# Local attention on one core: TensorE multiplies the values of chunk n-4 before it turns chunk n-3

## The reference, cut to what matters

```python
def _L0_attn_ref(x, wq, wkv, wo, q_norm_w, k_norm_w):
    q = x @ wq.T                      # 16 query heads of 64
    kv = x @ wkv.T                    # one key head, one value head
    ...
    q = _rmsnorm(_rope(q), q_norm_w)
    k = _rmsnorm(_rope(k), k_norm_w)
    mask = (cols <= rows) & (rows - cols <= WINDOW)     # WINDOW = 128
    scores = jnp.einsum('bqgtd,bqgsd->bqgts', q, k) * scale
    scores = jnp.where(mask[None, None, None], scores, NEG)
    attn = jax.nn.softmax(scores, axis=-1)
    out = jnp.einsum('bqgts,bqgsd->bqgtd', attn, v)
    ...
    return out @ wo.T
```

## Time and profile before

| | |
|---|---|
| median of three executions | 912.0 us (903.77 to 914.52) |
| the profiled execution | 905.44 us, of which the span of the instructions is 902.8 us |
| mean granted clock of TensorE | 0.900 of full speed |
| busy: PE, DVE, ACT, POOL | 739.3, 607.1, 448.7, 429.4 us |
| chunks of local attention | 4 images x 32 = 128 |

### The profile page before, as it was taken

The page is one execution under the profiler, slowest core; times in us unless marked ns, Lnnn a source line. Parts: engine busy times, 40 slices in busy tenths (PEclk is TensorE's granted clock), DMA queues, the critical chain, the costliest instruction groups (busy, mean ns, idle before and its releaser), DMA issues. The chain is left out here.

```text
span 902.8 us, 21152 instructions
## 1 busy us (share of the span) xinstructions
PE 739.3 (82%) x8196; PEld 484.5 (54%) x8196; DVE 607.1 (67%) x1209; ACT 448.7 (50%) x1405; POOL 429.4 (48%) x556
## 2 busy tenths in 40 slices
PE   6699999899998989988789979987899986405880
PEld 6243776426774447763267734773577753303660
DVE  0478887588885988876878836676577759512870
ACT  0024999127994359972299925312666650101100
POOL 0655666274662656643656612662033230472675
PEclk9889999999999999999999998997999997556755
DMA  7353000170000710001200000008000004017000
GB/s 253 118 204 73 3 3 3 46 219 14 2 4 1 233 45 3 3 3 29 62 2 3 3 1 1 1 3 110 8 3 2 2 2 129 27 44 129 9 18 14
DMA packets 60008, 41.30 MB, mean 46 GB/s; under 512 B 51760, under 2 KB 57389, under 8 KB 59124
## 3 DMA queue, kind: packets, MB, share of 16 engines
q1 hardware_dynamic: 57462, 33.03, 14.5%
q10 hardware_dynamic: 144, 4.19, 1.2%
q0 software_dynamic: 2304, 2.74, 0.9%
HBM read 25.44 MB, written 7.15 MB: 36 GB/s over the span
## 5 line engine op out<-in xcount | busy, mean ns | idle before, releaser
L795 ACT ACTIVATE work<-ps,small,rq 128x160 f32<-128x160 f32 x512 | 242.8, 487 | 31.9 <-DVE small L741 31.4
L774 POOL TENSOR_TENSOR work<-work,small 128x512 f32<-128x512 f32 x128 | 133.1, 1040 | 123.9 <-DVE small L758 123.9
L738 DVE TENSOR_REDUCE ps<-ps 128x4 f32<-128x640 f32 x128 | 106.5, 832 | 40.5 <-PE ps L648 39.2
L795 ACT ACTIVATION_READ_ACCUMULATOR work<-ps,small,rq 128x1 f32 x512 | 105.3, 206 | 0.0
L648 PE MATMUL ps<-kT,big 64*128 64x160 f32 x1024 | 97.8, 311 | 0.0
L750 DVE COPY pT<-ps 128x640 f32<-128x640 f32 x116 | 95.5, 823 | 0.5 <-issue 0.5
L683 PE MATMUL ps<-pT,vwin 128*64 128x128 f32 x1024 | 84.2, 282 | 9.7 <-ACT big L783 2.4
L273 PE MATMUL ps<-xT,s_proj_w 64*128 64x512 f32 x288 | 78.6, 663 | 12.6 <-PEq L213 7.5
L608 POOL TENSOR_TENSOR big<-prod 128x1024 f32<-128x1024 f32 x28 | 65.8, 2361 | 27.4 <-DVE prod L575 27.2
L648 PEld LDWEIGHTS ps<-kT,big 64*128 64x128 f32 x1024 | 76.1, 191 | 0.1
L683 PEld LDWEIGHTS ps<-pT,vwin 128*64 128x64 f32 x1024 | 56.7, 136 | 23.6 <-issue 17.6
(11 more groups left out here) (284 smaller groups left out, 1425.8 us busy)
## 6 DMA issues: line engine op xcount, KB each, us to landing
xb<-in_x SPq DMA_DIRECT2D x3, 4096.0 KB, 14.0
xb<-in_x ACTq DMA_DIRECT2D x1, 4096.0 KB, 18.0
vrem<-hl SPq DMA_DIRECT2D x64, 64.0 KB, 2.1
sent_rows<-empty_row SPq DMA_DIRECT2D x8, 325.0 KB, 9.9
s_proj_w<-in_proj_w SPq DMA_DIRECT2D x1, 1536.0 KB, 6.1
big<-sent_rows SPq DMA_DIRECT2D x5, 264.0 KB, 5.2
big<-sent_rows SPq DMA_DIRECT2D x5, 256.0 KB, 4.6
xb<-in_ffn_w SPq DMA_DIRECT2D x1, 1028.0 KB, 4.6
```

What stands on the lines that cost most here:

```text
L738: ch.step(v.tensor_reduce(row_max(c), ps[:, s_banks(c), 0:2 * SPAN].rearrange("p e (h k) -> p e h k", h=2), X, ALU.max))
L774: g.tensor_tensor(probs[:, c % 3, :, 0:P], probs[:, c % 3, :, 0:P], bc(small[:, c % 4, 3, :], P), ALU.mult)
L795: nc.scalar.activation(probs[:, c % 3, q, :], bank[2 * (c % 2) + e][:, SPAN * hh:SPAN * hh + SPAN], ACT.Exp, bias=small[:, c % 4, 1, q:q + ...
```

## The change

Inside PE's loop the two calls change places. No instruction is added or removed, and no wait either; the waits that belong to a call move with it. `values(n - 4)` now comes after `scores(n)`, and `turn(n - 3)` comes last.

```diff
                         pe.wait_ge(S["x_loaded"], 16 * VALUE_LOADS)
                         if b + 1 < IMAGES:
                             pe.wait_ge(S["next_kept"], 1)
+                    if n >= 4:
+                        values(n - 4)
                     if 3 <= n < CHUNKS + 3:
                         turn(n - 3)
-                    if n >= 4:
-                        values(n - 4)
                 pe.wait_ge(S["oT_ready"], CHUNKS)
```

## The result

The changed kernel takes 1030.71 us (median of four, 1029.45 to 1033.95), beside 912.84 for the kernel before (four executions, 903.77 to 914.52). The ratio is 1.134, with a 95% interval of 1.129 to 1.139. The profiled execution took 1031.31 us with a span of 1029.5, which is 126.7 more than the 902.8 before; 98 were forecast.

The account below looks back on a forecast made before the run. The prediction took ACT to bound the kernel's steady part, PE close behind. It added 4 x (21.8 + 0.2 + 2.5) = 98 us to the profiled 905.4, giving 1003.5, and named 1007 us, range 988 to 1035.

Parts of the forecast that it names:

- the loop: Local attention's steady part: a cycle of waits through PE and ACT, once a chunk, binds; 993 to 1020 us, chance 83%.
- the end of an image: From q0 of chunk 31 to the output projection: 10.50 us where it was 7.97, +2.5 an image.
- the step: Time from one chunk's q0 to the next, chunks 4 to 31: 2.99 us where 2.184 was, 21.8 us an image.
- ACT's idle time: Sign: ahead of q0 ACT idles some 0.8 us a chunk, put down to PE's turn.
- the first image's local attention: Sign: image 0's local attention longer by 24 us, the experts onward unchanged.
- PE's idle time: Sign: ahead of the values PE idles about 0.5 us a chunk, put down to ACT's output copy.
- The clock rival: Rival: PE's clock falls in the gaps of the steady chunks, +56 us, 1063 us; chance 10%.
- Chunks 0 to 4: Start of each image: q0 of chunk 4 also waits for values and turn; 0.2 us an image, 0.8 in all.
- Only PE's order costs: Rival: in the steady chunks no loop closes; 2.31 us a chunk, about 921 us; chance 4%.
- Not slower: Rival: the steady chunks stay at 2.184 us with ACT the bound, about 905 to 912 us; chance 3%.

Follow-up runs that it names:

- e1: Changed kernel with ACT's output copy ahead of q0, where it stood between q1 and q2; 950.12 us, ratio to before 1.050.
- e2: Changed kernel with four buffers for the exponentials in place of three, so q0 waits for the turn of n-4; 945.66 us, ratio 1.046.
- e3: Changed kernel with products that nothing reads in PE's gaps after the last scores of each image; 1010.63 us, ratio to before 1.119.
- e6: Kernel before up to n = 31, with the changed order (values first) only from n = 32 on; 933.38 us, ratio 1.025.
- e5: Changed kernel with the new order only for n from 4 to 31, the old order (turn first) after; 1004.23 us, ratio 1.102.

## Why the prediction was right in direction and too small

Forecast were 1007 us and, for the loop, 993 to 1020; measured were 1030.71. That lies in the wide range of 988 to 1035, and in the stretch that the prediction gave to a falling clock (1020 to 1118) with a chance of 10%. The step that failed is the end of an image: the prediction put it at 10.50 us with the clock at 1.00 and the projection behind it at no change. It took 13.86 us at a clock of 0.54, and the projections took 7.6 us more in sum. Of the signs that the prediction named, the step and ACT's idle time came true; the end of an image, and the first image's local attention, forecast 24 us longer and 29.8 longer from its first q0 to L714, did not.

**The mechanism** was right, piece by piece. The loop q0, q1, output copy, values, turn, q0 is what binds; the timeline shows its pieces at 1.32, 0.14, 0.96 and 0.63 against 1.31, 0.15, 0.97 and 0.56; and it went when either wait was met early (e1, e2), and shrank by one exponential when one was taken out of it. DVE's copy and the scores were covered, and ACT idles 0.81 ahead of q0, as forecast. PE's idle time was not: 0.91 us a step where some 0.5 was forecast, since the scores end 0.55 after q0 and not 0.9. That costs nothing by itself, but the argument on the clock rested on it.

**The step** was sized at 2.99 and measured 3.053. The whole difference is the last piece: the 0.56 had been read from ACT's half copy (L803), which waits for the turn first and for the values second. Ahead of q0 the turn is the second wait, and that costs 0.06. Exchanging the waits brought 2.993. Over 108 steps this is 6.5 us. The range allowed for it (3.06), the middle value did not. The wait list of the two instructions, not only the engine and the releaser, has to be alike where a hand-over is carried from one row to another.

**The end of an image** is the step that failed. The count of its rounds was right: with the clock held at 1.00 (e3) it takes 10.34 us, forecast 10.50. A round there takes 2.39 and not 2.50, mostly because the output copy starts 0.34 behind the half copy and not 0.44, and the first half copy starts 0.18 later than forecast. But the forecast put all of it at the full clock, and at 0.5 it takes 13.86, and the projection behind it, forecast unchanged, begins at the low clock and takes 2 us more. That is 12.6 us at the ends and about 7.5 behind them, 20 of the 28 us missed. e3 shows the cause: it only puts products, and one wait for the bank that they use, into PE's gaps, and the clock stays at 1.00. What e3 leaves open is how much the thinner steady steps ahead of the gap add to it.

**The clock rival** was placed wrongly. I looked for it in the steady loop, where PE waits 0.91 us in 3.05 and the clock stayed 1.00. There the argument against it was unsound and the outcome luck: I had PE busy 2.4 of 3 us, more than in the earlier trace rows, but it is busy 13.65 of 20, less than the 3.76 of 5 of those rows. And I argued from the kernel before's own ends, where gaps of 0.50 and 0.60 had left it at 1.00. The ends of the changed kernel have no scores between values and turn, and gaps of 1.56 and 0.90 that my own sum contained (1.46 behind q0 for the first values, then half copy, output copy and hand-over each time) and that I never held against those 0.50 and 0.60. The page "TensorE: Matmul & The Clock Gate" of the Trainium skill, whose section on queue depth-cycling speaks of short idle spells that make the clock swing, agrees with the ends in that short gaps brought the clock down (0.54 over the window), though it fell there once an image and did not swing, and not with the steady part (1.00).

**Chunks 0 to 4** cost 2.5 where I set 0.8. In three images the step from chunk 3 to 4 is 2.52 in place of 2.11, and the last image, in whose first chunks the clock is low for a while in both kernels, has 1.3 more in all. That the low clock makes the last one longer was not tried.

**The other rivals.** "Only PE's order costs" was sized at 2.31 a chunk, and I had missed that the loop through DVE (turn, copy, values, turn) is longer: 2.42 when the one through ACT is opened. It did not matter for the changed kernel, and it is the reason that opening the loop through ACT did not bring the step near 2.184. "Not slower" is out: the step did not stay at 2.184.

**The sum against the median.** The forecast of 1007 was 10.4% over the median before; the ratio is 1.134. What was missed is larger than the spread of the kernel before (903.77 to 914.52), so the miss is one of the terms above and not one of the runs.

## What to carry to other kernels

When two calls change places on one engine, write down which wait moves ahead of which result, and look whether the waited-for instruction itself waits, one pass earlier, for that result: here the loop through two engines cost its whole length a pass, and its pieces could be read off before, to within 0.06 us. Then look at the passes where part of the filling is missing, as at the end of a loop: here the gap was longest there (1.56 us against 0.91), TensorE's clock fell, and the projection behind it began slow. Where a wait that is surely late stands beside one that is surely met, put the late one first.

## What the runs showed of the hardware that I had not expected

The order of two waits ahead of one instruction costs time if the late one is the second: 0.06 us on ACT (step 3.053 to 2.993) and 0.09 us on PE (2.993 to 2.900). The clock held 1.00 with PE waiting 0.91 us in every 3.05 (100 to 120 us), and fell to 0.5 within the gap of 1.56 at the end of three images, in the fourth about 1 us after it. In e6, where the first gap is 1.11 to 1.17 and the later ones 0.90, with transposes and values alone between them, it fell between the first gap and just after the fourth. In e5 it fell in two of four images, and in e1 and e2 in five of eight, though the images of a run have the same instructions in this stretch, so whether it falls there is not settled by these instructions alone.
